# Attention with relative positions: the shifted rows of a pair of heads read back in one transfer of four tiles

## The reference

```
content_score = einsum('bhsp,bhtp->bhst', q + u, k)
pos_score = einsum('bhsp,htp->bhst', q + v, pos)
pos_score = _relative_shift(pos_score)
score = (content_score + pos_score) / sqrt(P)
weights = softmax(score, axis=-1)
out = einsum('bhst,bhtp->bhsp', weights, val)

def _relative_shift(x):          # x: (b, h, s, s)
    x = pad(x, ((0, 0), (0, 0), (0, 0), (1, 0)))
    x = x.reshape(b, h, s + 1, s)
    return x[:, :, 1:, :].reshape(b, h, s, s)
```

## Time and profile before

| | us |
|---|---|
| Three runs, median | 2155.24 |
| lowest and highest of them | 2147.13, 2161.48 |
| The profiled execution, its own time | 2169.97 |
| its span | 2168.2 |
| TensorE busy in the span | 2026.5 (93%) |
| VectorE | 1497.7 (69%) |
| ScalarE | 1286.9 (59%) |
| GpSimd | 1521.7 (70%) |

### The profile page before, as it was taken

The page is one execution under the profiler, slowest core; times in us unless marked ns, Lnnn a source line. Parts: engine busy times, 40 slices in busy tenths (PEclk is TensorE's granted clock), DMA queues, the critical chain, the costliest instruction groups (busy, mean ns, idle before and its releaser), DMA issues.

```text
span 2168.2 us, 84229 instructions
## 1 busy us (share of the span) xinstructions
PE 2026.5 (93%) x35763; PEld 1357.8 (63%) x35763; DVE 1497.7 (69%) x2268; ACT 1286.9 (59%) x1844; POOL 1521.7 (70%) x2307
## 2 busy tenths in 40 slices
PE   4888888887999999999999999999999999999997
PEld 1445555554666676666766677666776667666675
DVE  2444444447877877787777787777778778778772
ACT  3666666643566655666556565665656666566653
POOL 3343444448878887788877887778877788777880
PEclk8999999998999999999999999999999999999998
DMA  4999999952224222242222422224222243222231
GB/s 122 319 327 311 314 328 320 341 201 62 71 63 119 61 67 65 62 118 62 68 62 62 117 67 61 63 61 118 71 62 62 61 117 73 63 61 62 67 73 40
DMA packets 120004, 261.51 MB, mean 121 GB/s; under 512 B 29092, under 2 KB 34128, under 8 KB 118864
## 3 DMA queue, kind: packets, MB, share of 16 engines
q1 hardware_dynamic: 102224, 189.01, 31.9%
q10 hardware_dynamic: 17408, 67.11, 9.9%
HBM read 87.06 MB, written 68.29 MB: 72 GB/s over the span
## 4 chain that ended last, share of the span: by engine, by line
PE 66%; POOL 5%; DVE 4%; issue 2%; ACT 1%; POOLq 0%; DVEq 0%; ACTq 0%
PE ring L463 21%; PE ring L529 9%; PE ring L473 8%; PE yps L541 7%; PE ring L499 6%; PE ring L569 4%; PE ring L510 4%; PE tpose L579 3%; PE ring L491 1%; POOL roped L275 1%; DVE turned L643 1%; DVE ss L652 1%; PE tpose L551 1%; POOL ss L248 1%; DVE stats L701 1%
## 5 line engine op out<-in xcount | busy, mean ns | idle before, releaser
L643 DVE TENSOR_TENSOR turned<-ring,ropes 128x1024 f32<-128x1024 f32 x384 | 452.2, 1220 | 301.9 <-PE ring L463 301.9
L240 POOL TENSOR_TENSOR roped<-turned 128x512 f32<-128x512 f32 x384 | 521.8, 1385 | 171.3 <-PE ring L473 170.5
L463 PE MATMUL ring<-wqkv,xT 128*128 128x512 f32 x1152 | 568.2, 617 | 4.7 <-ACT xT L328 3.5
L275 POOL TENSOR_TENSOR roped<-roped,rnorm 128x1024 f32<-128x1024 f32 x192 | 361.5, 1904 | 7.5
L1152 POOL TENSOR_SCALAR less<-less,lowest 128x512 f32<-128x512 f32 x256 | 175.4, 697 | 262.7 <-DVE lowest L1121 262.7
L1121 DVE CUSTOM_DVE_ANT_0 less<-ps_b,shifted 128x512 f32<-128x512 f32 x256 | 166.7, 689 | 246.1 <-DMA shifted<-scratch_w 132.5
L463 PEld LDWEIGHTS ring<-wqkv,xT 128*128 128x128 f32 x1152 | 198.6, 192 | 161.5 <-issue 150.2
L369 ACT COPY pT<-ring 128x1024 f32<-128x1024 f32 x96 | 97.2, 1012 | 303.5 <-PE ring L510 303.5
L529 PEld LDWEIGHTS ring<-pT,vwin 64*64 64x64 f32 x12288 | 198.6, 134 | 52.3 <-issue 51.7
L317 ACT ACTIVATE squares<-ring 128x1024 f32<-128x1024 f32 x192 | 197.3, 1028 | 55.7 <-DVE turned L643 55.7
L529 PE MATMUL ring<-pT,vwin 64*64 64x32 f32 x12288 | 220.0, 220 | 5.0 <-issue 3.5
(11 more groups left out here) (133 smaller groups left out, 3232.4 us busy)
## 6 DMA issues: line engine op xcount, KB each, us to landing
vwin<-v SPq DMA_DIRECT2D x1536, 64.0 KB, 2.0
shifted<-scratch_w ACTq DMA_DIRECT2D x64, 1024.0 KB, 12.7
scratch_w<-wrows SPq DMA_DIRECT2D x48, 1026.0 KB, 11.8
scratch_w<-x SPq DMA_DIRECT2D x16, 1026.0 KB, 11.1
wqkv<-in_l_wqkv SPq DMA_DIRECT2D x6, 1536.0 KB, 6.8
wo<-in_l_wo SPq DMA_DIRECT2D x6, 512.0 KB
w<-in_l_w SPq DMA_DIRECT2D x6, 342.0 KB
w<-in_l_w SPq DMA_DIRECT2D x6, 171.0 KB
```

Of the source, the lines that this page charges most:

```text
L240: nc.gpsimd.tensor_tensor(halves[2][:, :, side, :], halves[0][:, :, side, :], halves[1][:, :, 1 - side, :], ALU.add).then_inc(s[name + "_a ...
L275: nc.gpsimd.tensor_tensor(whole, whole, norm, ALU.mult).then_inc(s[name + "_roped"], 1)
L463: last = nc.tensor.matmul(out[:, half, :], xT[:, t % SEQT * P:(t % SEQT + 1) * P], wqkv[:, layer_of(t), at + half * 512:at + (half + 1) * ...
L643: ins = nc.vector.tensor_tensor(turned[:, n, part, :].rearrange("p (h d) -> p h d", d=DH), heads, table, ALU.mult)
```

## The change

The two reads of a pair of heads become one read of all four tiles, 128 partitions x 2 heads x 8,192 bytes, 2,048 KB. There are three buffers of four tiles in place of six of two (the same bytes). The read of pair n is issued in round 4n + 8. The content scores run 14 rounds behind the position scores in place of 12. DVE waits for a read in every fourth round. SP waits, ahead of a write to a place used before, for one read in place of two.

```diff
-            LAG, READ_AT = 12, 8
-            NW, NR = 4, 6
+            LAG, READ_AT = 14, 8
+            NW, NR = 4, 3
...
-            shifted = sb2("shifted", [P, NR, 2, 2, S])
+            shifted = sb2("shifted", [P, NR, 2, STEPS, S])
...
                         if n // 2 >= KEPT:
-                            for done in range((n // 2 - KEPT) * 2, (n // 2 - KEPT) * 2 + 2):
-                                sp.wait_ge(read[done % NR], in_slot(read, done))
+                            done = n // 2 - KEPT
+                            sp.wait_ge(read[done % NR], in_slot(read, done))
...
-                            if c % 2 == 0:
-                                dve.wait_ge(read[c // 2 % NR], in_slot(read, c // 2))
+                            if c % STEPS == 0:
+                                dve.wait_ge(read[c // STEPS % NR], in_slot(read, c // STEPS))
...
-                                    less[:, c % 2, k, :], ps[:, 2 + k, :], shifted[:, c // 2 % NR, k, c % 2, :], -SCALE0, HIGHEST,
+                                    less[:, c % 2, k, :], ps[:, 2 + k, :], shifted[:, c // STEPS % NR, k, c % STEPS, :], -SCALE0, HIGHEST,
...
-                        n = (r - READ_AT) // 2
-                        if r % 2 == 0 and 0 <= n < ROUNDS // 2:
-                            u, i, g = of(2 * n)
-                            for done in range(n // 2 * 2, n // 2 * 2 + 2):
+                        n = (r - READ_AT) // STEPS
+                        if r % STEPS == 0 and 0 <= n < ROUNDS // STEPS:
+                            for done in range(2 * n, 2 * n + 2):
                                 act.wait_ge(written[done % NW], in_slot(written, done))
-                            at_least(act, s["c_taken"], 4 * (n - NR + 1))
-                            src = flat[place(n // 2):place(n // 2) + 2, S:(S + 1) * S].rearrange("h (p i t) -> p h i t", i=STEPS, t=S)
-                            act.dma_start(shifted[:, n % NR, :, :, :].rearrange("p h i t -> p h (i t)"),
-                                          src[:, :, i:i + 2, :].rearrange("p h i t -> p h (i t)")).then_inc(read[n % NR], 16)
+                            at_least(act, s["c_taken"], 2 * STEPS * (n - NR + 1))
+                            src = flat[place(n):place(n) + 2, S:(S + 1) * S].rearrange("h (p c) -> p h c", p=P)
+                            act.dma_start(shifted[:, n % NR, :, :, :].rearrange("p h i t -> p h (i t)"), src
+                                          ).then_inc(read[n % NR], 16)
```

## The result

The changed kernel takes 2185.56 us in the median of four runs (2180.87 to 2186.24), the kernel before 2156.76 us beside it: a ratio of 1.0131, 95% interval 1.0111 to 1.0152. It is **slower by 29 us**, 1.3%. The forecast was 2161 us and no change that can be told; the range, 2126 to 2188, held the result near its upper end. The size is nearly that of the second rival (2188 us).

The account below looks back on a forecast made before the run. It took DMA writes to DRAM, near their limit, to set the block's pace. Only the longer lag counted, +6.0 us, all other terms 0; on the 2155.2 us median that gave 2161 us, range 2126 to 2188.

Parts of the forecast that it names:

- second rival: DMA queues: turns by packet lengthen stretches of writes alone, making ACT's write wait late; 27 us more, 2188 us, chance 0.17.
- its chance (0.18): Whole kernel: the chance given to a result slower by more than 1%, 21.6 us.
- the lag: Content rounds: two more rounds of lag cost their time once, at the end or start, +6.0 us.
- the prediction's own signs: Block that changes: four rounds in 12.8 to 13.2 us, about 325 GB/s; wrong at 12.2 or less, 13.6 or more.
- The writes are so near the limit that they and not the reads set the pace: DMA writes to DRAM: 162 GB/s written, against about 186 GB/s if writes go on; earlier reads priced at 0.
- first rival: DMA read queue: one long, earlier read ends most slow stretches; 41.6 us back in full, 2120 us, chance 0.20.
- Most waits of DVE for a read should end ... ACT will: Six rounds of lead end most of DVE's 127.7 us of read waits; ACT waits for writes instead, 0 us.
- Reads get two thirds: DMA engines taking turns by packet: doubled read packets move at 271 GB/s, costing writes 1.3 us, within the spare time.
- The fixed cost of a transfer: DMA: the skill's about 2.0 us each would give back up to 64 us for 32 fewer transfers; forecast rejected it.
- Packets of 8,192 bytes: Read queue q10: packets of 8,192 bytes for 4,096, half as many.
- A byte costs the same: DMA packets: 38.6 ns for 1,000 bytes at either packet size, so larger packets change 0 us.
- Content round 0 at 67 to 69 us: Start of content rounds: the first begins at about 68.1 us in place of 61.55, 6.56 us later.

Follow-up runs that it names:

- e2: The kernel before with a lag of 14 rounds in place of 12, reads still of two tiles: ratio 1.0144 to the kernel before.
- e5: The changed kernel with position scores forced to the other row group wherever they would meet content scores: 2143.13 us against 2152.57 for the kernel before, ratio 0.9952.
- e6: The kernel before with position scores forced into the content scores' row group in half of the rounds: 2185.81 us, ratio 1.0163.
- e8: The kernel before with lag 14, two-tile reads, and position scores forced to the other row group where they would collide: 2136.00 us against 2149.42, ratio 0.9928.
- e9: The kernel before with lag 14, five buffers, and operands copied 64 partitions further so no scores meet, reference's results: 2144.30 us against 2152.88, ratio 0.9963.
- e10: The kernel before with lag 13, two-tile reads, and operands copied 64 partitions further for one round in four, reference's results: 2143.84 us, ratio 0.9958.
- e1: The changed kernel with the lag put back to 12 rounds, reads of four tiles kept: 19.4 us slower than the kernel before, ratio 1.0091.
- e7: The changed kernel with a lag of 13 rounds, so one round in four has both scores in one row group: 2166.72 us, ratio 1.0073.

## Why the prediction was right and wrong

The range held the time and the way the time went had its chance (0.18). That is luck: the range reached 2188 for the sake of the second rival, and the 29 us have another cause. The forecast missed by 24.6 us, because a part had no line in it: **the lag was costed as two rounds more and nothing else, "+6.0, ends 5.7 and 6.6"**. The price of a round was taken from the rows of lag 12 and held to be the same at 14. It isn't: two of four rounds lost 0.8 us each. TensorE's operations were neither added nor removed, only moved against each other, and the step never asked what ran beside what. e2 shows it with the lag alone, e5 and e6 with the lag held. Of the prediction's own signs, four rounds at 13.42 us are over the 12.8 to 13.2 named and short of the 13.6 that was to prove it wrong, and the second stretch moved 303 GB/s and not 325.

- **"The writes are so near the limit that they and not the reads set the pace": wrong.** At the cadence of e8 the writes go at 2.10 MB in 12.03 us, 175 GB/s, and the share of 1.02 was no proof of a full bound: 356 GB/s go through at the same share. e8's 12.03 us are also under the 12.2 that the prediction named as the sign that the writes are no limit. But 175 is still under the 186 GB/s of the earlier trace rows: whether writes can go faster than that for long, no run shows. The fall ahead of the first read is in all ten traces without the copies of e9 and e10. From 45 to 50 us the first writes run alone in the kernel before (first line) and in e2 (second line), whose first four writes are issued within 0.2 us of the same times:

```profile
DMA packets 223, 0.85 MB, mean 170 GB/s; under 512 B 16, under 2 KB 16, under 8 KB 223
DMA packets 269, 1.04 MB, mean 208 GB/s; under 512 B 16, under 2 KB 16, under 8 KB 269
```

  e1, e6 and e7 moved 213, 207 and 213 GB/s there. So the slow stretches come again, but the traced execution of the kernel before was the slowest of them, and the rate near 186 is partly its own. What sets them off is open.

  The first rival had it nearer: an earlier read ends the waits. It was priced at 41.6 us from the single four rounds of the earlier trace rows; with all that belongs to a unit (turned outputs, projections) e8 runs at 12.03 and not 11.68 us, which leaves (12.99 - 12.03) x 127 / 4 = 30.5 us against the traced execution. In the medians e8 gains 13.4 us, with its two rounds more paid for.
- **"Most waits of DVE for a read should end ... ACT will": half right.** They ended, 127.7 to 25.6 us, the one at the start. ACT did not take them over (its waits for a write are 8.7 us in two); the wait for TensorE did.
- **"Reads get two thirds": right where both queues run, but they seldom do.** From 64 to 67 us of the changed kernel the packet counts are even and the bytes are not, 0.90 of 1.27 MB for the reads:

```profile
DMA packets 216, 1.27 MB, mean 424 GB/s; under 512 B 16, under 2 KB 16, under 8 KB 106
...
q10 hardware_dynamic: 110, 0.90, 70.8%
q1 hardware_dynamic: 106, 0.37, 30.3%
```

  That is the turn at packet granularity that the Trainium skill gives (DMA: Bandwidth & Descriptors, Queues, rings and completion order), as the prediction cites it, and that the earlier trace rows could not tell from a turn by bytes. Later one queue mostly runs behind the other: from 213.7 to 216.2 us, behind the issue of a write at 213.72 us, only the read's packets run:

```profile
DMA packets 115, 0.94 MB, mean 377 GB/s; under 512 B 0, under 2 KB 0, under 8 KB 0
...
q10 hardware_dynamic: 115, 0.94, 99.5%
```

  The second rival's mechanism, longer stretches of writes that delay ACT, played no part in the changed kernel's time: writes landed sooner than before (8.2 and 9.0 us in the median where the earlier trace rows have 11.8 and 11.1), and e5 and e6 move the time without touching a transfer. At the faster pace of e5 the writes do land later (13.9 and 14.5 us); whether that costs e5 something against e8 is not shown.
- **The fixed cost of a transfer: nothing came back, as forecast.** e5 has 32 transfers fewer than e8 and is no faster (0.9952 and 0.9928), so the estimate of up to 64 us is not seen. The fit that the prediction took from the Trainium skill (DMA: Bandwidth & Descriptors, Anatomy of one DMA) is stated there for transfers that GpSimd issues; the ones here are issued by SP and ACT.
- **Packets of 8,192 bytes: right**, 8,704 packets on q10 for 67.11 MB where there were 17,408. **A byte costs the same: right** within a tenth. From 64 to 67 us a read's packet takes 0.708 x 16 x 3 / 110 = 0.309 us, 37.7 ns for 1,000 bytes; from 213.7 to 216.2 us it takes 0.995 x 16 x 2.5 / 115 = 0.346 us, 42.2 ns, where the prediction had 38.6.
- **Content round 0 at 67 to 69 us: 64.2 us**, four us early. Seen from the start the longer lag cost 2.7 us (61.5 to 64.2) and not 6.6; the sum was not saved by it.
- **The total against the trace.** Spans differ by 16.2 us, and DVE's last content operation by the same 16.2 us (474.6 and 490.8): all of it is in this block. The medians differ by 28.8 us, because the profiled execution before was 13.2 us over its median. Taking the price of late reads from it was the other weak point: part of the 12.99 us for four rounds probably belongs to that execution, and no trace of a typical one is at hand.

## What to carry to other kernels

Before a software pipeline is shifted by some rounds, write down for each round which two operations will stand side by side, and which rows of the array, banks and buffers each takes; what meets depends on the lag's remainder (here by 8, since the row groups repeat every eight rounds) and not only on its length. A price read from a trace holds for a neighbour as well as for an operation. And a DMA share of 1.0 says that something is queued, not that no more bytes fit: only a run in which the consumer asks for more tells.

## What was not expected of the hardware

- Four matmuls of 32 rows and 512 columns in float32, in four different groups of 32 rows, start within 0.02 us and are done in 1.07 us; with two in each of two groups they take 1.92 us (the changed kernel's timeline above).
- With the DMA share at 1.01 to 1.02 in all of them, the same stretch from 166 to 270 us moved 301 GB/s (e2), 313 (before) and 356 to 357 (e8, e5).
- In the changed kernel a write issued at 213.72 us behind a read of 256 packets had no packet under way 2.5 us later, though the two are on different queues; the write issued at 206.36 us, with the read queue empty, began about 0.9 us behind its issue. Yet from 64 to 67 us the two queues took turns. What decides between the two is open.
- Writes alone, at a DMA share over 1.0, slow down after some us: in e2 from 296 GB/s (40 to 45 us) to 208 (45 to 50 us), in the kernel before from 248 to 170.
